# Nine NF4 chunks as one stream through the attention loop of a cross-attention and FFN kernel

## The reference, cut to what matters

```python
x = x + xattn(layernorm(x), ctx, ctx, mask, Wq, Wk, Wv, Wo)
x = x + ffn(layernorm(x), w1, w2, w3)

# xattn: 32 query heads, 8 key/value heads, head size 128
q, k = rope(query @ Wq), rope(key @ Wk);  v = value @ Wv
logits = 30 * tanh(q k^T * 0.0884 / 30), masked;  out = softmax(logits) v @ Wo

# ffn: each weight is first quantised to NF4 and back
flat = w.reshape(-1, 64)                       # blocks of 64
absmax = max(|flat|) per block
idx = searchsorted(15 bounds, flat / absmax)   # 16 code values
dq = NF4_CODE[idx] * absmax
out = (silu(x dq1^T) * (x dq2^T)) dq3^T
```

## Time and profile before

| What | Value |
|---|---|
| Time, median of 3 runs | 920.55 us (914.53 to 921.25) |
| Time of the profiled execution | 916.73 us |
| Its span, first to last instruction | 914.8 us |
| Mean granted TensorE clock | 0.962 |
| Busy: PE | 818.3 us (89%) |
| Busy: DVE | 669.7 us (73%) |
| Busy: ACT | 466.7 us (51%) |
| Busy: POOL | 446.3 us (49%) |

### The profile page before, as it was taken

The page is one execution under the profiler, slowest core; times in us unless marked ns, Lnnn a source line. Parts: engine busy times, 40 slices in busy tenths (PEclk is TensorE's granted clock), DMA queues, the critical chain, the costliest instruction groups (busy, mean ns, idle before and its releaser), DMA issues.

```text
span 914.8 us, 10681 instructions
## 1 busy us (share of the span) xinstructions
PE 818.3 (89%) x3806; PEld 650.5 (71%) x3806; DVE 669.7 (73%) x743; ACT 466.7 (51%) x571; POOL 446.3 (49%) x272
## 2 busy tenths in 40 slices
PE   6688893999999999999998998997779797994998
PEld 4576782677788777777886776775567686883886
DVE  3777752788888898888887987888766589698120
ACT  4014742565565656555655655655332576677100
POOL 1645056556857758659659568474102223253000
PEclk9899997999999999999999999999799999998999
DMA  9564735333433423435325234213013013120210
GB/s 328 151 188 140 209 92 169 90 81 93 144 92 90 126 79 114 123 81 155 81 70 167 58 92 144 57 48 101 1 32 133 24 35 114 32 76 23 84 58 35
DMA packets 63540, 91.75 MB, mean 100 GB/s; under 512 B 6784, under 2 KB 30464, under 8 KB 63488
## 3 DMA queue, kind: packets, MB, share of 16 engines
q1 hardware_dynamic: 63488, 91.07, 34.1%
HBM read 51.00 MB, written 19.07 MB: 77 GB/s over the span
## 4 chain that ended last, share of the span: by engine, by line
PE 51%; POOL 15%; DVE 13%; DMA 8%; issue 6%; ACT 5%; SPq 2%; POOLq 0%; DVEq 0%; ACTq 0%
POOL qT L1149 6%; PE bank L463 5%; PE bank L465 4%; PE bank L464 4%; DMA sw<-cs_loop 4%; PE bank L558 4%; PE bank L497 3%; PE bank L499 3%; PE bank L498 3%; PE bank L481 3%; PE bank L482 3%; PE bank L483 3%; PE avp L569 3%; DMA sw<-cs_start 3%; PE trp L470 2%
## 5 line engine op out<-in xcount | busy, mean ns | idle before, releaser
L1149 POOL TENSOR_TENSOR qT<-cs_loop,sw 128x512 f32<-128x512 f32 x58 | 92.6, 1597 | 104.9 <-DMA sw<-cs_loop 99.8
L763 ACT ACTIVATE eb<-bank 128x512 f32<-128x512 f32 x64 | 38.3, 598 | 194.4 <-PE bank L558 194.4
L890 DVE SCALAR_TENSOR_TENSOR nfa<-nfp,nfa 128x1408 f32<-128x1408 uint8 x56 | 106.8, 1907 | 32.5 <-ACT nfp L702 31.2
L890 DVE SCALAR_TENSOR_TENSOR nfv<-nfp,nfv 128x1408 f32<-128x1408 uint8 x56 | 106.5, 1902 | 28.0 <-ACT nfp L702 26.8
L1215 POOL TENSOR_TENSOR eb<-eb,maskf 128x512 f32<-128x512 f32 x64 | 91.1, 1425 | 62.4 <-ACT eb L765 62.4
L702 ACT ACTIVATE nfp<-nfv,bnd 128x1408 uint8<-128x1408 f32 x75 | 107.0, 1460 | 20.4 <-POOL nfv L1165 15.8
L497 PE MATMUL bank<-woh,ath 128*128 128x512 f32 x256 | 109.4, 427 | 0.0
L481 PE MATMUL bank<-xh,wqh 128*128 128x512 f32 x256 | 106.5, 416 | 0.0
L499 PE MATMUL bank<-woh,atl 128*128 128x512 f32 x256 | 103.2, 403 | 0.0
L498 PE MATMUL bank<-wol,ath 128*128 128x512 f32 x256 | 103.0, 402 | 0.0
L890 DVE SCALAR_TENSOR_TENSOR nfx<-nfp,nfx 128x1408 f32<-128x1408 uint8 x42 | 79.9, 1902 | 30.2 <-ACT nfp L702 30.2
(11 more groups left out here) (134 smaller groups left out, 1814.4 us busy)
## 6 DMA issues: line engine op xcount, KB each, us to landing
sw<-cs_loop SPq DMA_DIRECT2D x116, 128.0 KB, 2.3
stage<-wq_pieces SPq DMA_DIRECT2D x32, 256.0 KB, 2.9
stage<-wo_pieces SPq DMA_DIRECT2D x32, 256.0 KB, 2.9
stage<-dq_scratch SPq DMA_DIRECT2D x32, 256.0 KB, 3.2
sw<-cs_start SPq DMA_DIRECT2D x44, 128.0 KB, 2.4
ks_scratch<-qT SPq DMA_DIRECT2D x16, 256.0 KB, 2.3
vs_scratch<-vst SPq DMA_DIRECT2D x16, 256.0 KB, 3.3
kcur<-ks_scratch SPq DMA_DIRECT2D x16, 256.0 KB, 3.2
```

Of the source, the lines that this page charges most:

```text
L890: op = nc.vector.scalar_tensor_tensor(acc[:, :], nfp[:, n % 2, :], STEPS[i], acc[:, :], ALU.mult, ALU.add)
L1149: nc.gpsimd.tensor_tensor(dst, products(ru, slot)[:, 0, :], sw[:, slot, :], ALU.add).then_inc(roped, 1)
```

## The change

Five things change. (a) `nf_sequence` makes one stream of chunks 1 to 9 of 144 places (15 levels and one place for the next chunk's `nf_prepare` per chunk); `nf_head(j)` hands out 33 places per 14 steps over steps 0 to 55, and 12 over the last 8. The FFN keeps chunks 10 and 11, two levels per unit, from unit 1 to unit 16. (b) The load of x and of chunk 0 goes from SP's queue to ACT's. (c) The first chunk's 15 levels take 11 steps of the V phase instead of 13, its store goes behind the exchanges of the V phase, and `nf_rescale(0)`, `nf_prepare(1)`, `nf_normalise(1)` and `mask(0)` move up. (d) PE's first logits go ahead of query unit 5. (e) SP's program of the loop is written as one pattern per step, and the stores, loads and the places of buffers follow the stream.

```diff
             with ExitStack() as loop:
+            nfx = sb("nfx", [128, CH], f32, loop)
             cs_loop = sb("cs_loop", [128, 2, 2, 512], f32, loop)
-            nfx = sb("nfx", [128, CH], f32, loop)
...
         def nf_bufs(c):
-            if c > NKV:
-                return [(nfa, nfy), (nfv, nfa), (nfy, nfv)][c - NKV - 1]
+            if c > NKV + 1:
+                return [(nfv, nfy), (nfa, nfv)][c - NKV - 2]
...
         def nf_values(v):
-            return range(15 * v // 13, 15 * (v + 1) // 13) if v < 13 else range(0)
+            return range(15 * v // 11, 15 * (v + 1) // 11) if v < 11 else range(0)
...
+        def nf_sequence(lo, hi, first):
+            steps = [(first + p // 16, p % 16) for p in range(lo, hi)]
+            adds = [(c, r if r < 12 else r - 1) for c, r in steps if r != 12]
+            return adds, [c + 1 for c, r in steps if r == 12], [c for c, r in steps if r == 15]
+        def nf_head(j):
+            lo, hi = [33 * i // 14 if i <= 56 else 132 + 12 * (i - 56) // 8 for i in (j, j + 1)]
+            return nf_sequence(lo, hi, 1) if 0 <= j < NSTEP else ([], [], [])
         def nf_ffn(n):
-            return [divmod(k, 15) for k in range(45 * (n - 2) // 21, 45 * (n - 1) // 21)] if n >= 2 else []
+            lo, hi = [2 * (i - 1) for i in (n, n + 1)]
+            return nf_sequence(max(0, lo), min(hi, 32), NKV + 2)
-        def nf_head(kv, b):
-            if kv == NKV - 1:
-                return [[0, 1], [2, 3], [4, 5, 6], [7, 8], [9, 10], [11], [12], [13, 14]][b]
-            return [[0, 1], [2, 3], [4, 5], [6, 7], [8, 9], [10, 11], [12], [13, 14]][b]
...
 # SP
-            sp.dma_start(y[:, :, :], x_d.rearrange("b s d -> s b d")).then_inc(x_in, 16)
-            nf_load(0)
             for u in range(NK):
                 swap(u, u % 2)
...
             for v in range(16):
-                if v == 13:
+                if v == 12:
                     nf_load(1)
-                if v == 14:
-                    nf_store(0)
...
                 if u is not None:
                     query_swap(u)
+            nf_store(0)
...
+                    for c in nf_head(j - 2)[2]:
+                        nf_store(c)
+                    for c in nf_head(j - 3)[2]:
+                        nf_load(c + 2)
+                    if j == 1:
+                        nf_load(2)
...
             for n in range(4, 2 * HT):
-                if n == 15:
-                    nf_store(NKV + 1)
-                if n == 17:
+                if n == 6:
                     nf_load(NKV + 3)
+                if n == 18:
+                    nf_store(NKV + 2)
                 weights_in(n)
...
 # PE
                 if u is not None:
                     pe.wait_ge(xt_lo, 8)
+                    if v == 15:
+                        logits(0)
                     q_unit(u)
...
-            logits(0)
             logits(1)
...
 # ACT
             for n in range(16):
                 first_hi(n)
+                if n == 9:
+                    act.dma_start(y[:, :, :], x_d.rearrange("b s d -> s b d")).then_inc(x_in, 16)
+            act.dma_start(nfv[:, :], nf_d[:, 0:CH]).then_inc(nf_in, 16)
...
-                    bounds = nf_head(kv, b)
-                    for i in bounds[0:1]:
-                        nf_above_bound(kv + 1, i)
+                    adds = nf_head(j)[0]
+                    for c, i in adds[0:1]:
+                        nf_above_bound(c, i)
...
-                    for i in bounds[1:]:
-                        nf_above_bound(kv + 1, i)
+                    for c, i in adds[1:]:
+                        nf_above_bound(c, i)
...
 # DVE
-            nf_prepare(1)
+                if v == 14:
+                    nf_prepare(1)
...
-                    bounds = nf_head(kv, b)
-                    before = max(1, len(bounds) - 1)
-                    for i in bounds[:before]:
-                        nf_add(kv + 1, i)
-                    if b == 6 and not last:
-                        nf_prepare(kv + 2)
+                    adds, prepares, _ = nf_head(j)
+                    before = max(1, len(adds) - 1)
+                    for c, i in adds[:before]:
+                        nf_add(c, i)
+                    for c in prepares:
+                        nf_prepare(c)
                     u = j + AHEAD
                     if u < NUNIT:
                         rope_parts(NK + u, u % 2, csq[:, :, :])
-                    for i in bounds[before:]:
-                        nf_add(kv + 1, i)
+                    for c, i in adds[before:]:
+                        nf_add(c, i)
...
 # POOL
             for u in range(AHEAD):
+                if u == 5:
+                    nf_normalise(1)
+                    mask(0)
                 query_rope(u)
...
-                if u == 3:
+                if u == 1:
                     nf_rescale(0)
-            nf_normalise(1)
+            mask(1)
...
-                    if b == 7 and not last:
-                        nf_normalise(kv + 2)
-                    if b == 0 and kv > 0:
-                        nf_rescale(kv)
+                    for c in nf_head(j - 1)[2]:
+                        nf_rescale(c)
...
+                    for c in nf_head(j)[1]:
+                        nf_normalise(c)
```

More of the change, by code:

```diff
@@ L375, in head @@
                 last = kv == NKV - 1
[L376 to L408, removed]
-                if last:
-                    sp.wait_ge(nf_out, nf_stored(NKV - 1))
-                    for n in range(4):
-                        weights_in(n)
-                    nf_load(NKV + 1)
+                for b in range(B):
+                    j = 8 * kv + b
+                    head_piece(j + 3)
+                    if b == 0 and kv > 0:
+                        wait(sp, av_done, j)
+                        sp.dma_start(vcur[:, 4:8, 0:DH], vs_d[kv, 1]).then_inc(v_in[1], 16)
+                    if b == 4 and not last:
+                        wait(sp, av_done, j)
+                        sp.dma_start(vcur[:, 0:4, 0:DH], vs_d[kv + 1, 0]).then_inc(v_in[0], 16)
+                    query_swap(j + AHEAD)
+                    if b in (1, 5) and not last:
+                        wait(sp, logits_done, j + 3)
+                        sp.dma_start(kcur[:, b // 4, :], ks_d[kv + 1, b // 4]).then_inc(k_in[b // 4], 16)
+                    for c in nf_head(j - 2)[2]:
[4 more added lines that the diff above has]
+                        nf_load(2)
+                    if last and b == 3:
+                        sp.wait_ge(nf_out, nf_stored(NKV - 1))
+                        for n in range(4):
+                            weights_in(n)
@@ L534, in _, with logits @@
                     first_transposes(u - 10)
+            def logits(j):
+                kv, h, s = j // B, j % B // 4, j % 4
+                if s == 0:
+                    pe.wait_ge(roped, NK + 8 * kv + 4 * h + 4)
+                    pe.wait_ge(k_in[h], 16 * kv + 16)
+                wait(pe, tanh_done, j)
+                nc.tensor.matmul(lgp[:, :], kcur[:, h, s * 128:(s + 1) * 128],
+                                 qT[:, h, :, s * 128:(s + 1) * 128], start=True, stop=True).then_inc(logits_done, 1)
             for v in range(16):
@@ L548, in _ @@
                     pe.wait_ge(xt_lo, 8)
+                    if v == 15:
+                        logits(0)
                     q_unit(u)
-            def logits(j):
-                kv, h, s = j // B, j % B // 4, j % 4
-                if s == 0:
-                    pe.wait_ge(roped, NK + 8 * kv + 4 * h + 4)
-                    pe.wait_ge(k_in[h], 16 * kv + 16)
-                wait(pe, tanh_done, j)
-                nc.tensor.matmul(lgp[:, :], kcur[:, h, s * 128:(s + 1) * 128],
-                                 qT[:, h, :, s * 128:(s + 1) * 128], start=True, stop=True).then_inc(logits_done, 1)
             def weighted_values(j):
@@ L1200, in query_rope @@
                 rope(NK + u, u % 2, qT[:, half, g, :])
-            for u in range(AHEAD):
-                query_rope(u)
-                if u in (1, 3):
-                    for n in (28 + u - 1, 29 + u - 1):
-                        low(n % 4, woh0[:, n % 4, :], wol0[:, n % 4, :], n)
-                if u == 3:
-                    nf_rescale(0)
-            nf_normalise(1)
             def mask(j):
@@ L1217, in mask @@
                                         ALU.mult).then_inc(weights_done, 1)
+            for u in range(AHEAD):
+                if u == 5:
+                    nf_normalise(1)
+                    mask(0)
+                query_rope(u)
+                if u in (1, 3):
+                    for n in (28 + u - 1, 29 + u - 1):
+                        low(n % 4, woh0[:, n % 4, :], wol0[:, n % 4, :], n)
+                if u == 1:
+                    nf_rescale(0)
+            mask(1)
             def head(kv):
@@ L1238, in head @@
                         power(2, range(2, 4))
-            mask(0)
-            mask(1)
             for kv in range(NKV):
```

47 lines of the change are left out of this document (23 added, 24 removed).

## The result

The changed kernel takes 937.02 us (median of 4 runs, 930.45 to 939.75), the kernel before 917.54 us beside it (4 runs, 914.02 to 921.25). The ratio is 1.020, 95% interval 1.013 to 1.028: **slower, by some 2%**, where 905 us was forecast and the range ended at 920. Its profiled execution took 930.45 us, with a span of 928.6 for 914.8 before.

What follows compares the result with a forecast made beforehand. PE was taken to bound the loop, the chain PE -> ACT -> DVE -> PE 0.76 us behind. Terms: +37.1 (steps 0 to 57), -7.5, -7.5, +1.4, -14.3, -22.1, together -12.9: 903.8 profiled, 905 us forecast, range 884 to 920.

Steps and rivals of the forecast that it cites:

- Chunk borders (gain): Loop: rescaling, store wait and next normalisation no longer on adjacent steps, so late ropes go; -10 us, bounds 0 and 12.5.
- Maxima ahead of pressing ropes: Loop steps 5, 25, 53: maxima ahead of rope_parts make a wanted rope 1.3 to 1.5 us late; +4.5 us.
- Steps with three levels: Fifteen loop steps: twelve ordinary +25.2 us, three before logits needing their rope +11.4, low clock in those three +6.
- K phase: Start: x in ACT's queue lets the first exchange go sooner; -7.5 us, bounds 0 and 9.1.
- rival B: K phase: first exchange stays late because x and chunk 0 still move then; no gain, 911 us; chance 0.15.
- V phase and into the loop: Before the loop: doubled level at V step 2 costs +1.4 us; earlier exchange, rope, normalisation and mask give -14.3.
- Last head: Loop's end: fewer levels in steps 58 and 60, no low clock in step 59; -7.5 us.
- FFN: FFN: a chunk fewer and chunk 10 normalised in the loop remove three PE waits; -22.1 us with clock.
- Rival C: Loop: each of the fifteen three-level waits drops PE to the low clock; +23, 928 us; chance 0.11.
- Rival A: Loop: totals decide and DVE has the time, so a three-level step costs at most 0.5 us; 869 us; chance 0.12.

Runs made afterwards that it cites:

- pool_small: third_small with POOL's normalising of chunks 2 to 9 and rescaling of chunks 1 to 8 in the loop also cut to 64 columns; 880.78 us, ratio 0.960.
- x_only: The kernel before, with only the loads of x and chunk 0 moved from SP's queue to ACT's; 917.12 us, ratio 1.0003.
- third_small: The changed kernel, with the middle level (sign and DVE instruction) of each three-level step cut to 64 columns; 905.13 us, ratio 0.989.
- the early sign: The changed kernel, with ACT's second sign of every step moved ahead of tanh and exp; 893.73 us, ratio 0.976.
- both_sp: The kernel of both, with x and chunk 0 loaded from SP's queue again; 872.57 us, ratio 0.952.
- start_only: The kernel before, with only the change's edits up to the loop; loop and FFN as before; 903.78 us, ratio 0.986.
- both: The changed kernel, one level ahead of rope_parts, second sign ahead of tanh and exp, chunk borders and some third levels moved off pressing ropes; 870.17 us, ratio 0.949.

## Why the prediction was wrong, point by point

**The step that failed is "Chunk borders (gain)".** I credited 10 us because the three border operations no longer fall on adjacent steps, and called POOL's load outside the chain, as it was 49% busy. Instead the borders cost: without the third levels the loop is 32 us over that of before, 22 of it from POOL's normalising and rescaling (pool_small). Before, these lie in steps 7 and 0 of each head, and the rope of step 1 comes late, by 1.0 us in four heads and 2.5 in two. In the stream they drift against the heads, and fall into or just ahead of steps 13, 21, 29, 33, 41 and 49. Counted by place, from `ath` to `ath` against the same steps of before, the changed kernel loses 10.1 us in steps that have no third level, neither their own nor one just before them, and no maxima ahead of a pressing rope; my sum had a gain of 10 there. (In x_only's trace of the old loop these steps differ by 0.1 us from before.)

The way in which the borders cost is, by the rows of the changed kernel, mostly not the backlog of POOL that I had expected when I made pool_small; no run separates the two. Of the 14 ropes that PE waits for in the changed kernel, POOL starts only two (steps 29 and 49) late by its own queue, 3.9 us behind the end of the products; for the other twelve it stands idle until the exchange is there, 3.0 behind it. There the products are late, and in 13, 33 and 41 they are later than the chain makes them because a level meets POOL's operation: the ten levels of the loop that start while POOL normalises or rescales take 2.91 us on average, for 1.6 alone (before, 14 such levels took 2.37). My sum had DVE's and POOL's operations at their rows' prices, as if neither could touch the other.

**Maxima ahead of pressing ropes (+4.5)** was too small: 7.4 us by place in the changed kernel, 9.4 in pool_small, less what scatters in step 25. In step 5 of pool_small the level ahead of the maxima took 2.35 us for 1.6, and the two small instructions behind them 1.2 us together for the 0.5 that I had estimated.

**Steps with three levels (+25.2, +11.4, +6).** The twelve ordinary ones held in mechanism and size: the first is 9.70 us for 9.8 forecast, and by place they and the steps behind them cost 25.2 us, 22.5 of which go with the third levels (third_small). The three that precede a pressing rope cost 16.2 us by place for 17.4 forecast, and that is luck: taking the third level away gives back only 5.7 of it, and 10.6 go with POOL's border operations (pool_small). PE's waits for these three ropes are 6.19, 4.56 and 4.58 us, for 3 to 4 forecast. The steps took 15.4, 13.5 and 13.9 us from `ath` to `ath`, and without the third level still 10.8, 11.3 and 13.5. In the whole loop the third levels gave 28 us for my 42.6. Split by what is taken away first, these shares differ, since the waits overlap; the early sign took 39 us from the same loop.

**K phase (-7.5)** failed: nothing measurable. It is rival B in mechanism. POOL's first rope starts at 20.51 us in the changed kernel, where I had asked for 17, and its V phase starts 2.7 us ahead. Even this is not shown to come from the queue: both_sp, with SP's queue, starts it 1.7 us ahead of before, and the traces with ACT's queue differ among themselves by 4 us (73.7 to 77.7). That term is most of the 6 us missing at the start. **V phase and into the loop (+1.4, -14.3)** held, by start_only: -12 to -13. **Last head (-7.5)** gave -9.9, **FFN (-22.1)** gave -22.5.

Rival C was added up wrongly: its +23 is its whole change against the profiled execution, 916.73 us, and I put it on top of 905. By its own terms it is 941 us on the runs' scale, not 928. So it came nearer in time than it says, and is wrong in its reason: the three-level steps between 178 and 263 us, with waits of up to 1.8 us, left the clock at 1.00; the low stretch shown goes with 6.19 us, a wait for rope. Over the whole profiled execution the granted clock is 0.971, for 0.962 before. Rival A is wrong for this kernel, where signs and not totals decided. In "both" the totals do nearly suffice: 7.82 us in a three-level step.

## What to carry to other kernels

When work is spread evenly over a loop, look up where its irregular parts (a border's preparation, a rescaling) will fall against the loop's own deadlines, step by step on each engine; an engine that is half busy on average can still come in the way where it counts, by its own queue or by slowing another engine's instruction on the pressing chain. And before moving work off a chain, look for the instruction that closes the chain too late: here one ACT instruction a step, moved ahead of two others, was worth some 40 us, and made the order on DVE indifferent. Place it ahead of everything that waits for the same event, not just ahead of the last wait.

## What the runs showed of the hardware

I had priced levels and POOL's operations by their rows alone. In step 13 the level that started 0.5 us behind a normalisation took 3.53 us: it ended at 270.35, 1.5 behind that operation's end at 268.87. The low part, started at 268.83, took 2.67 and ended 1.15 behind the level. In "both" it is the mask that takes 2.68 beside a level of 1.61. So of two such operations the second seems to stand until the first has ended, rather than both slowing. The Trainium skill says so ("SBUF — State Buffer", section "Who interferes with whom"): a DVE operation with two SBUF inputs and a GpSimd operation that reads SBUF take turns, and the one issued second waits in full. These rows agree with it; no run here was made to test it. In the changed kernel a level of DVE on average took 1.94 us over 154 (nfv, nfa and nfx together) for 1.6 alone; before it was 1.90, so most of this was there already, and what is new is where it falls.
